# One kernel, four layers on one core: the router's logits as four column groups and one transpose, its weights turned in one transpose, and the outputs added one pair earlier

## What is computed

```python
x = x + attn_a(layernorm(x))   # 16 heads, squared-relu attention, tanh-normalised outputs
x = x + ffn(layernorm(x))      # 32 experts, 8 chosen per token, and one shared expert
x = x + attn_b(layernorm(x))   # softmax over 32 taps, out[l] = sum_d w[l, d] * x[l + d]
x = x + ffn(layernorm(x))      # the same experts again

# ffn: flat is [T, 128], gate_w [32, 128], experts [32, 64, 128]
logits = flat @ gate_w.T
scores = sigmoid(logits)
# 8 groups of 4 experts; the 4 groups with the largest sums stay; top 8 experts of these
combine = top8(masked scores), divided by their sum          # [T, 32], zero elsewhere
out = sum_e combine[:, e] * ((silu(flat @ wg[e].T) * (flat @ wu[e].T)) @ wd[e].T) + shared(flat)
```

## Time and profile before

| | |
|---|---|
| runs of the kernel before | 561.87 us median of 3 (561.01 to 563.82) |
| the profiled execution | 564.94 us, span 563.0 us from the first to the last instruction, mean granted TensorE clock 0.985 of full speed |
| PE busy | 530.1 us, 94% of the span |
| DVE busy | 425.2 us, 76% |
| ACT busy | 376.3 us, 67% |
| POOL busy | 327.3 us, 58% |
| unit 0 (with the end of attention) | 229 to 281 us |
| unit 1 | 281 to 318 us |
| units 2 to 5 (with the tap layer) | 318 to 484 us |
| units 6, 7 | 484 to 563 us |

### The profile page before, as it was taken

The page is one execution under the profiler, slowest core; times in us unless marked ns, Lnnn a source line. Parts: engine busy times, 40 slices in busy tenths (PEclk is TensorE's granted clock), DMA queues, the critical chain, the costliest instruction groups (busy, mean ns, idle before and its releaser), DMA issues.

```text
span 563.0 us, 10120 instructions
## 1 busy us (share of the span) xinstructions
PE 530.1 (94%) x3280; PEld 400.5 (71%) x3280; DVE 425.2 (76%) x1006; ACT 376.3 (67%) x676; POOL 327.3 (58%) x276
## 2 busy tenths in 40 slices
PE   5788799999999998899999999999999999999997
PEld 4555467676666665586877787787787888888885
DVE  5966868787879687449849869769769768677675
ACT  6687958677779775364466776776775775755644
POOL 2743929384846564077646756646656656566563
PEclk9899989999999999699999999999999999999999
DMA  8200000000000012910085480650751751761920
GB/s 227 86 16 14 23 15 17 15 15 15 16 16 15 15 24 64 225 30 1 6 199 103 111 197 26 171 137 24 187 123 29 183 122 48 180 139 38 223 62 19
DMA packets 36099, 44.73 MB, mean 79 GB/s; under 512 B 5456, under 2 KB 18896, under 8 KB 36048
## 3 DMA queue, kind: packets, MB, share of 16 engines
q1 hardware_dynamic: 31360, 42.40, 31.7%
q10 hardware_dynamic: 4688, 1.71, 1.3%
HBM read 40.94 MB, written 3.15 MB: 78 GB/s over the span
## 4 chain that ended last, share of the span: by engine, by line
PE 69%; DVE 11%; issue 7%; ACT 7%; POOL 3%; DMA 1%; SPq 0%; ACTq 0%; DVEq 0%; POOLq 0%
PE PS L1220 66%; DVE aT L866 4%; DVE n L845 3%; POOL hl L499 2%; ACT sqv L547 2%; ACT v L540 2%; ACT rl L565 1%; DMA Osb<-wa_dram 1%; PE PS L1355 1%; DMA wbc<-w_dram 1%; PE PS L1341 1%; DVE wfl L911 0%; PE PS L1474 0%; PE PS L1313 0%; ACT n2T L581 0%
## 5 line engine op out<-in xcount | busy, mean ns | idle before, releaser
L499 POOL TENSOR_TENSOR hl<-hb,hh 128x512 fp32r<-128x512 f32 x127 | 164.3, 1294 | 133.7 <-ACT hh L709 129.5
L702 ACT ACTIVATE sil<-PS 128x512 f32<-128x512 f32 (+1 forms) x136 | 80.8, 594 | 82.8 <-PE PS L1220 82.0
L1087 DVE TENSOR_TENSOR PS<-sil,PS 128x512 f32<-128x512 f32 x128 | 88.3, 690 | 61.0 <-PE PS L1220 39.1
L1220 PE MATMUL PS<-fxh,wfh 128*128 128x512 f32 x264 | 105.2, 398 | 3.1 <-issue 1.7
L1220 PE MATMUL PS<-fxl,wfh 128*128 128x512 f32 x264 | 105.0, 398 | 0.0
L1220 PE MATMUL PS<-fxh,wfl 128*128 128x512 f32 x264 | 104.7, 397 | 0.0
L709 ACT ACTIVATE hh<-hb 128x512 fp32r<-128x512 f32 x128 | 80.3, 627 | 32.5 <-DVE hb L1092 30.7
L1092 DVE TENSOR_TENSOR hb<-PS,wbc 128x512 f32<-128x512 f32 x128 | 88.5, 691 | 9.3 <-issue 3.2
L866 DVE SCALAR_TENSOR_TENSOR aT<-PS,rl 128x1024 f32<-128x1024 f32 x64 | 75.2, 1217 | 7.7 <-ACT rl L565 7.6
L565 ACT ACTIVATE rl<-PS 128x1024 f32<-128x1024 f32 x64 | 62.1, 1026 | 21.9 <-PE PS L1220 21.8
L424 POOL TENSOR_TENSOR sr<-n2o,half 128x32 f32<-128x32 f32 x7 | 38.2, 5462 | 51.5 <-DVE n2o L873 51.5
(11 more groups left out here) (175 smaller groups left out, 902.7 us busy)
## 6 DMA issues: line engine op xcount, KB each, us to landing
wbc<-w_dram SPq DMA_DIRECT2D x48, 512.0 KB, 11.6
wbc<-w_dram SPq DMA_DIRECT2D x32, 128.0 KB, 2.9
wbc<-w_dram SPq DMA_DIRECT2D x16, 256.0 KB, 4.2
wfs<-wf_dram SPq DMA_DIRECT2D x32, 98.0 KB, 2.0
band_dram<-zero SPq DMA_DIRECT2D x16, 80.0 KB, 1.7
band<-band_dram ACTq DMA_DIRECT2D x4, 320.0 KB, 3.1
X<-x_dram SPq DMA_DIRECT2D x1, 896.0 KB, 7.7
Osb<-wa_dram SPq DMA_DIRECT2D x3, 256.0 KB, 3.7
```

Source lines behind the costliest of these rows:

```text
L499: g.tensor_tensor(hl[:, n % RING, :], hb[:, n % RING, :], hh[:, n % RING, :].bitcast(F32), ALU.subtract).then_inc(F("hl"), 1)
L702: s.activation(sil[0:rows, n % 2, :], PS[0:rows, G0 + n % 2, :], ACT.Silu).then_inc(F("silu"), 1)
L1087: v_.tensor_tensor(PS[:, bank, :], sil[:, n % 2, :], PS[:, bank, :], ALU.mult).then_inc(F("t"), 1)
L1220: return nc.tensor.matmul(o, w, m, start=start, stop=stop)
```

## The change

`prep_logits` makes each product the other way round: the router's weights `gw` (32 columns) are stationary and the 128 tokens of a tile move, and the four tiles write to partitions 0, 32, 64, 96 of one bank. The result has tokens along the free axis, so ACT copies it to `lT` (`prep_keep_logits`, which is now what frees `pl`), and PE turns it with one 128x128 transpose into a new job `pt` (`prep_turn_logits`), one pair later. `prep_scores` reads `pt` one pair later than it read `pl`, and frees `pt`. `pt` stands in bank MB between `pl` and `fo`. `prep_combine` is one transpose of 128x128 instead of four of 128x32, and `wTs` is copied from 128x128 and written to DRAM with four DMAs. `transpose_sum` and `add_experts` move from pair 6 to pair 5, `mix_apply` and `add_mix` from pair 13 to pair 12, `group_scores` from 5 to 6 (in unit 0 from 6 to 7), `choose_groups` in unit 0 from 7 to 8.

```diff
--- before.py
+++ after.py
@@ -93,7 +93,7 @@
     order += [("g", 0, j) for j in range(2, NQ)] + [("xT", 1)]
     for b in range(B):
         n, q, r = b + 1, b - 1, b - 2
-        order += late(r, ("F", r, 2), ("F", r, 3))
+        order += late(r, ("F", r, 2), ("F", r, 3)) + ([("pt", 0)] if b == B - 1 else [])
         order += coming(n, ("qk", n, 0), ("qk", n, 1), ("v", n, 0, 0), ("v", n, 0, 1)) + late(q, ("nb", q))
         order += coming(n, ("v", n, 1, 0)) + late(q, ("nt", q)) + coming(n, ("v", n, 1, 1))
         order += ([("px", 0)] if b == B - 2 else []) + ([("pc", 0)] if b == B - 1 else []) + late(r, ("y", r, 0))
@@ -115,6 +115,7 @@
         if u + 1 < NU:
             turns.add(MB, "px", u + 1)
             turns.add(MB, "pl", u + 1)
+            turns.add(MB, "pt", u + 1)
         if u:
             turns.add(MB, "fo", u - 1)
         if 2 <= u < NC + 2:
@@ -197,7 +198,8 @@
         winv = sb("winv", [P, CT])
         wsel = sb("wsel", [P, CT, E])
         comb = sb("comb", [P, CT, E])
-        wTs = sb("wTs", [E, CH])
+        lT = sb("lT", [P, P])
+        wTs = sb("wTs", [P, P])
 
         PS = ctx.enter_context(nc.psum_tensor("PS", [P, 8, 512], F32))
 
@@ -346,8 +348,9 @@
                 sp.wait_ge(*freed("pc", u))
                 for k in range(len(PARTS) - 1):
                     after(sp, F(f"bc{k}"), 32 * (u - 1))
-                sp.dma_start(wdram[u % 2, :, :], wTs[:, :]).then_inc(F("wput"), 16)
-                sp.wait_ge(F("wput"), 16 * (u + 1))
+                for t in range(CT):
+                    sp.dma_start(wdram[u % 2, :, t * P:(t + 1) * P], wTs[t * E:(t + 1) * E, :]).then_inc(F("wput"), 16)
+                sp.wait_ge(F("wput"), 16 * CT * (u + 1))
                 after(sp, F("h"), pair(u - 1, 0))
                 if u == 0:
                     sp.wait_ge(*full("g", B - 1, NQ - 1))
@@ -610,17 +613,23 @@
                 s.activation(x32[:, :], PS[:, bank_of("px", u), :], ACT.Copy).then_inc(F("p_x32"), 1)
                 s.activation(fxh[u % 2][:, :], PS[:, bank_of("px", u), :], ACT.Copy).then_inc(free_of("px", u), 1)
 
+            def prep_keep_logits(u):
+                act.wait_ge(*full("pl", u))
+                if u:
+                    act.wait_ge(*full("pt", u - 1))
+                s.activation(lT[:, :], PS[:, bank_of("pl", u), 0:P], ACT.Copy).then_inc(free_of("pl", u), 1)
+
             def prep_scores(u):
-                act.wait_ge(*full("pl", u))
-                s.activation(th0[:, :], PS[:, bank_of("pl", u), 0:CT * E], ACT.Tanh, scale=0.5).then_inc(free_of("pl", u), 1)
-                act.wait_ge(*freed("pl", u))
+                act.wait_ge(*full("pt", u))
+                s.activation(th0[:, :], PS[:, bank_of("pt", u), 0:P], ACT.Tanh, scale=0.5).then_inc(free_of("pt", u), 1)
+                act.wait_ge(*freed("pt", u))
                 after(act, F("p_ms"), u)
                 s.activation(sc[:, :], th0[:, :], ACT.Copy, bias=0.5, scale=0.5).then_inc(F("p_sc"), 1)
 
             def prep_weights(u):
                 act.wait_ge(*full("pc", u))
-                after(act, F("wput"), 16 * u)
-                s.activation(wTs[:, :], PS[0:E, bank_of("pc", u), :], ACT.Copy).then_inc(free_of("pc", u), 1)
+                after(act, F("wput"), 16 * CT * u)
+                s.activation(wTs[:, :], PS[:, bank_of("pc", u), 0:P], ACT.Copy).then_inc(free_of("pc", u), 1)
 
             tokens_high(0)
             first_weights_high(2)
@@ -643,6 +652,8 @@
                 n, q = b + 1, b - 1
                 more, last = n < B, b == B - 1
                 relu(NG * b + 1)
+                if last:
+                    prep_scores(0)
                 if more:
                     square_pairs(n, 0)
                     square_pairs(n, 1)
@@ -692,7 +703,7 @@
                 if b == B - 3:
                     prep_normalise(0)
                 if b == B - 2:
-                    prep_scores(0)
+                    prep_keep_logits(0)
 
             def gate(u, p):
                 n = pair(u, p)
@@ -782,6 +793,8 @@
                         if p == (3 if first else 2):
                             prep_tokens(u + 1)
                         if p == (5 if first else 4):
+                            prep_keep_logits(u + 1)
+                        if p == (6 if first else 5):
                             prep_scores(u + 1)
                         if p == (15 if first else 13):
                             prep_weights(u + 1)
@@ -1181,12 +1194,12 @@
                             mix_weights(u - 2)
                         if p == 10:
                             mix_halo(u - 2)
-                        if p == 13:
+                        if p == 12:
                             add_mix(u - 2)
                     if u + 1 < NU:
-                        if p == (6 if first else 5):
+                        if p == (7 if first else 6):
                             group_scores(u + 1)
-                        if p == 7:
+                        if p == (8 if first else 7):
                             choose_groups(u + 1)
                         if p == (9 if first else 8):
                             mask_scores(u + 1)
@@ -1194,7 +1207,7 @@
                             choose_experts(u + 1)
                         if p == (12 if first else 10):
                             combine(u + 1)
-                    if p == 6 and u:
+                    if p == 5 and u:
                         add_experts(u - 1)
                     if p == 12 and 1 <= u <= NC:
                         mix_stats(u - 1)
@@ -1345,15 +1358,18 @@
                 pe.wait_ge(F("p_x32"), u + 1)
                 bank, done = turn("pl", u)
                 for t in range(CT):
-                    last = mm(PS[:, bank, t * E:(t + 1) * E], x32[:, t * P:(t + 1) * P], gw[:, :], True, True)
+                    last = mm(PS[t * E:(t + 1) * E, bank, 0:P], gw[:, :], x32[:, t * P:(t + 1) * P], True, True)
                 last.then_inc(done, 1)
+
+            def prep_turn_logits(u):
+                pe.wait_ge(*freed("pl", u))
+                bank, done = turn("pt", u)
+                nc.tensor.transpose(PS[:, bank, 0:P], lT[:, :], ident[:, :]).then_inc(done, 1)
 
             def prep_combine(u):
                 pe.wait_ge(F("p_comb"), u + 1)
                 bank, done = turn("pc", u)
-                for t in range(CT):
-                    last = nc.tensor.transpose(PS[0:E, bank, t * P:(t + 1) * P], comb[:, t, :], ident[:, :])
-                last.then_inc(done, 1)
+                nc.tensor.transpose(PS[:, bank, 0:P], comb[:, :, :].rearrange("p t e -> p (t e)"), ident[:, :]).then_inc(done, 1)
 
             pe.wait_ge(cs("id"), 1)
             transpose_tokens(0)
@@ -1382,6 +1398,8 @@
                 score(NG * b + 1)
                 if r >= 0:
                     spread_factors(r, 1)
+                if last_batch:
+                    prep_turn_logits(0)
                 if more:
                     pe.wait_ge(*freed("xT", n))
                     pairs(n, 0)
@@ -1553,9 +1571,11 @@
                             prep_transpose(u + 1)
                         if p == (5 if first else 4):
                             prep_logits(u + 1)
+                        if p == (6 if first else 5):
+                            prep_turn_logits(u + 1)
                         if p == (14 if first else 12):
                             prep_combine(u + 1)
-                    if p == 6 and u:
+                    if p == 5 and u:
                         transpose_sum(u - 1)
                     if 2 <= u < NC + 2:
                         if p == 2:
```

## The result

| | before | changed |
|---|---|---|
| median (lowest to highest), 20 runs each | 561.94 us (559.34 to 563.82) | 568.85 us (563.87 to 571.71) |
| ratio, 95% interval | | 1.0111 (1.0085 to 1.0137) |
| profiled execution | 564.94 us, span 563.0 | 569.98 us, span 568.1 |
| unit 0, from its first gate matmul to unit 1's | 51.97 us | 47.96 us |
| unit 1 | 37.47 us | 41.26 us |

The change costs 6.9 us on the medians; 6.1 was forecast. Unit 0 was shorter in this execution because the clock at its start, 0.55 in the profile of before, was 1.00 here. That differs from one execution to the next: 22 of the 80 later runs of before have a mean granted clock of 0.996 or 0.997, which leaves no room for such a stretch, and two profiles of kernels with the new logits have 0.70 there.

The account below looks back on a forecast made before the run. PE's matmuls bound the kernel from unit 1. + 8.1 (new wait) + 0.0 (unit 0) - 6 x 0.33 (`comb`) = + 6.1 us on 561.87 gave 568.0 us; own range 565.5 to 570.5, with clock 564.8 to 573.5.

Parts of the forecast that it names:

- logits slot: The logits products in PE's queue: from 0.89 to 0.6 us, a saving of 0.3; ends 0.25 and 0.85.
- `comb` slot: The transposes of `comb` on PE: one instead of four, 0.44 to 0.11 us, saving 0.33 us.
- part 3: New wait of PE at pair 5, units 1 to 6, until the Tanh frees `pt`: 8.1 us lost.
- unit 0, `choose_groups`: Moved to pair 8, before DVE's next `hidden`: its 0.77 us, hidden before, now stands on the path, + 0.8.
- cover before pair 9: PE's wait for POOL's `hl`, units 2 to 5: 1.1 us of the new wait counted as already paid.
- Part 1: Logits by four column groups: slot 0.6 us instead of 0.89, a saving of 0.3 us.
- four changes of tile: Entering and leaving another tile shape, read from `mix_apply`: 0.17 us each; two on top give the logits' high end, 0.85.
- Part 4: Unit 0 and attention: + 0.8 for `choose_groups` against savings from logits and `comb`, together + 0.0.
- Part 5: Moved `mix_apply` and `add_mix`, four DMA issues (0.9 us added), one more ACT copy: put at no cost.
- Absorption: Rival: the wait at pair 5 is given back at once, DVE or POOL setting the pace; 558.8 us, chance 0.06.
- The clock's fall in unit 1: Rival: the new 2.6 us wait there lowers PE's clock, costing 5 us; 573.0 us, chance 0.14.
- The wait of 1.38 us: Unit 0, PE waiting for DVE at 264.00: cited because it did not lower the clock.

Follow-up runs that it names:

- e11: The changed kernel run again, unaltered: 569.49 us, ratio 1.0162.
- e8: Changed kernel with outputs at pair 6, one DMA, `mix_apply` at 13, `choose_groups` at 7 in unit 0, `comb` at 13 in units 2 to 5: 560.10 us.
- e7: The kernel before with the four logits products made twice: 568.16 us, ratio 1.0112.
- e1: The changed kernel with `transpose_sum` and `add_experts` back at pair 6: 562.82 us, ratio 1.0027.
- e3: The changed kernel with the Tanh of the scores ahead of `hidden_high` in ACT's queue: 564.28 us, ratio 1.0028.
- e2: The kernel before with only `transpose_sum` and `add_experts` at pair 5, `mix_apply` and `add_mix` at pair 12: 562.71 us, ratio 1.0006.
- e5: The changed kernel with the combine weights written to DRAM by one DMA instead of four: 568.61 us, ratio 1.0127.
- e6: The kernel before with only `comb` turned by one transpose and written by four DMAs: 561.24 us, ratio 0.9989.
- e9: The changed kernel with the spread combine weights cut so that pair 4 comes in a smaller part, 768 KB instead of 1 MB: 567.62 us, ratio 1.0111.

## Why the prediction was right

The sign, the place and the mechanism were right, and the sum was near: 6.1 us forecast, 6.9 measured. That it is so near is in part luck, as unit 1 and the clock below show. Term by term, in the profiles of the changed kernel (the second number is e11's):

| term | forecast | measured |
|---|---|---|
| logits slot | 0.6 us (0.25 to 0.85) | 499.38 - 498.68 - 0.23 = 0.47; 0.55 by the length of the pair |
| `comb` slot | 0.11 | 0.11 (pair 12 of unit 1 takes 2.21, others 2.10) |
| part 3, unit 6, with `comb` | + 0.3 | + 0.5 and + 1.1 |
| part 3, units 2 to 5, with `comb` | + 3.6 | + 3.8 and + 3.8 |
| part 3, unit 1, with `comb` | + 2.3 | + 3.8 and + 1.9 |
| units 1 to 6 together | + 6.1 | + 8.1 and + 6.8 |
| unit 0, `choose_groups` | + 0.8 | + 0.5 in pair 11 (4.43 against 3.95), 0.6 against e8 (3.85) |
| cover before pair 9 | 1.1 in all | 1.06 (e7) |

**Part 1** was nearest to its row of column groups. The four changes of tile of 0.17 us that I read off are not seen again: sixteen records took 1.00, and eight with half the columns 0.47. This is also above 0.22 us, a quarter of 0.89, the estimate by the Trainium skill's "Up to 4×" (TensorEngine Tiling (Array Packing), Theoretical Speedup). For the total neither matters: in units 1 to 5 what PE saves ahead of its wait is lost in it.

**Part 3** held in units 2 to 5 to 0.2 us, cover included. e1 and e3 show both halves of the mechanism, the bank and ACT's queue; e2 shows that it takes both moves.

**Unit 1 was mis-sized** in its spread: I took one landing of pair 4's weights as a constant. It lies anywhere between 12.6 and 14.6 us, and with it PE's wait between 1.3 (e5) and 3.4 us. In before PE ran ahead of it and did not wait. This may be one reason why the changed kernel's runs lie 7.8 us apart and those of before beside it 4.5.

**Part 4** was near for what it named: from pair 2 on, unit 0 is 0.2 us longer where the terms behind that point give 0.3. But the 0.3 us for `comb` in unit 0 was not gained: pair 14 is 0.3 shorter and pair 16 0.3 longer. And the wait of 1.86 us, which it saw coming, costs another 1.0 us when the clock falls behind it (e11).

**Part 5 was wrong in one place.** The four issues cost 1.70 us, not 1.2, and I took the lead of the reads over the unit as the cover. In unit 6 that did not hold for pair 4, the first pair of a part of 1 MB: DVE waited 1.7 us where it had not, and 2.3 in e11. Most of the lead was lost to `mix_apply` at pair 12, which I had put at no cost, and not to the four DMAs (e5, e2, e6). PE's wait in unit 6 was 0.87 and 1.45 us, against 0.66 where pair 4's weights came nearly in time (e5, e9): 0.2 and 0.8 us.

**The rivals.** Absorption fell (e7) where I had put it, on PE's free time, but is partly true for gains: in units 2 to 5 e1 gave back 2.9 of 5.2 us, where 1.1 was foreseen. The clock's fall in unit 1 did occur, in one of two profiles, and cost 1.3 us, not the 5 us that I had priced. Pair 5 of unit 1 took 7.19 us; less 2.10 for the pair, 0.74 for the transposes (what is left beside pair and wait in e5, e9 and e11) and 3.35 of waiting, 1.0 us is left, and pair 6 took 0.3 more than the others. The wait of 1.38 us that I cited against a fall was the one that the change itself lengthened to 1.86, and there the clock fell in four of seven profiles.

## What to carry to other kernels

Where jobs take turns in one bank, the price of a move isn't in the job moved but in who frees the slot in front of it: look up that instruction's place in its engine's queue and what stands ahead of it. A job needs a pair's distance from the release it waits for, and two small moves that are free one by one can use up the same distance. A late transfer that nobody feels is a debt; a new wait on an engine that ran ahead makes it due.

## What the runs showed of the hardware

The granted clock was 0.57 and 0.61 over 4 us behind stretches in which PE was busy 1.86 and 2.14 of 4 us, and stayed at 1.00 behind one in which it was busy 1.46 of 4 us (e11). So a wait of 1.9 to 3.4 us may or may not cost the clock, and which it is changes from one execution to the next: the same wait of 1.84 to 1.93 us in unit 0 cost it in four of seven profiles.

In before the mean clock of an execution goes with its time: over its 80 runs beside the experiments those with 0.996 or 0.997 took 559.2 to 560.7 us, those with 0.984 or 0.985 563.1 to 565.9. At 0.997 the changed kernel took 563.9 us against 559.5 (medians of 2 and 21 runs), at 0.996 565.0 against 560.7 (2 and 1): 4.4 and 4.3 us more. Its mean over all runs is 0.989, that of before 0.991, an estimated 1.1 us of 569. So the clock accounts for about one of the 2.5 us between 4.4 and 6.9; for the rest no run shows a cause. The varying wait of unit 1 is the nearest.
